# Softplus of the scan stage summed in PSUM by TensorE and copied out by ScalarE

## What is computed

```
x_conv = silu(conv(x_ssm) + conv_b)
dt = softplus(x_conv @ dt_w.T + dt_b)
dA = exp(dt[:, :, None] * A)
h = h * dA + (dt[:, :, None] * Bt[:, None, :]) * xt[:, :, None]      # 512 steps, 16 states per channel
y = einsum('bdn,bn->bd', h, Ct) + xt * D
```

## Time and profile before

| | us |
|---|---|
| median of 3 runs | 1474.12 |
| lowest, highest | 1471.44, 1475.02 |
| the profiled execution, its own time | 1474.04 |
| its span, first to last instruction | 1472.2 |
| first scan starts, last scan starts | 47.7, 673.6 |

### The profile page before, as it was taken

One profiled execution on the slowest core, in us unless ns is written; L12 is line 12 of the kernel. 1 busy time (PEld: TensorE's weight loads), 2 busy tenths in 40 slices (PEclk: granted clock), 3 DMA queues, 4 the chain that ended last, 5 costly groups with the idle time before them and its releaser, 6 DMA issues. The chain is left out here.

```text
span 1472.2 us, 17914 instructions
## 1 busy us (share of the span) xinstructions
PE 1198.7 (81%) x5074; PEld 801.4 (54%) x5074; DVE 1098.6 (75%) x1659; ACT 857.1 (58%) x1354; POOL 778.2 (53%) x519
## 2 busy tenths in 40 slices
PE   7778787887959687666139999999999999999950
PEld 3323243333424243323138888888888888888850
DVE  2889898989888898995427777777777777777743
ACT  3664646565654746431127677677767777776744
POOL 0356556777867686876632444444444444444452
PEclk8899789898968898886559999999999999999985
DMA  1443333544444443432464566556556565555537
GB/s 67 191 149 134 115 130 124 173 158 151 141 154 137 139 163 131 149 117 82 175 227 144 152 155 161 147 156 159 155 148 155 158 156 155 158 157 149 156 42 231
DMA packets 69254, 217.13 MB, mean 147 GB/s; under 512 B 7520, under 2 KB 43232, under 8 KB 56288
## 3 DMA queue, kind: packets, MB, share of 16 engines
q1 hardware_dynamic: 29664, 167.42, 31.6%
q0 software_dynamic: 26880, 36.72, 14.7%
q10 hardware_dynamic: 12672, 12.58, 2.6%
HBM read 165.54 MB, written 51.15 MB: 147 GB/s over the span
## 5 line engine op out<-in xcount | busy, mean ns | idle before, releaser
L511 PE MATMUL p_y<-read,small 128*128 128x512 f32 x512 | 297.3, 714 | 126.8 <-POOL read L1006 126.8
L850 DVE TENSOR_TENSOR_SCAN state<-decay,p_bu 128x1024 f32<-128x1024 f32 x128 | 292.3, 2283 | 33.6 <-ACT decay L677 27.9
L1432 POOL DMA_INDIRECT total<-o_v,tok x144 | 266.5, 1851 | 45.1 <-issue 44.8
L677 ACT ACTIVATE decay<-dt,scan_rate 128x511 f32<-128x511 f32 x256 | 169.2, 712 | 176.2 <-DVE state L850 175.9
L511 PEld LDWEIGHTS p_y<-read,small 128*128 128x128 f32 x512 | 104.9, 220 | 293.0 <-POOL read L1006 193.8
L1430 POOL TENSOR_TENSOR scrap<-neg_half 128x1 f32<-128x1 f32 x36 | 14.6, 405 | 356.3 <-ACT o_v L1317 353.8
L1006 POOL TENSOR_TENSOR read<-state,bc 128x1024 f32<-128x1024 f32 x64 | 150.5, 2351 | 52.4 <-DVE p_bu L841 20.3
L1294 ACT ACTIVATE gate_v<-p_g,bias 128x512 f32<-128x512 f32 x144 | 98.2, 682 | 97.1 <-PE p_up L1243 96.9
L1304 ACT ACTIVATE ah<-a_v 128x512 fp32r<-128x512 f32 x144 | 91.2, 633 | 91.7 <-DVE a_v L1378 91.7
L1006 POOL TENSOR_TENSOR read<-state,first_wh 128x1024 f32<-128x1024 f32 x32 | 75.4, 2355 | 109.7 <-DVE p_bu L841 87.8
L1367 DVE TENSOR_SCALAR up_v<-up_v 128x512 f32<-128x512 f32 x144 | 61.9, 430 | 63.7 <-ACT up_v L1297 63.6
(11 more groups left out here) (209 smaller groups left out, 3007.9 us busy)
## 6 DMA issues: line engine op xcount, KB each, us to landing
bc<-bc_rows SPq DMA_DIRECT2D x32, 1024.0 KB, 5.1
first_raw<-in_w_experts SPq DMA_DIRECT2D x19, 1668.0 KB, 6.7
raw_w<-in_w_experts SPq DMA_DIRECT2D x18, 1668.0 KB, 6.8
first_wh<-bc_rows SPq DMA_DIRECT2D x16, 1024.0 KB, 5.2
first_wl<-bc_rows SPq DMA_DIRECT2D x16, 1024.0 KB, 5.0
first_rows<-queues SPq DMA_DIRECT2D x19, 544.0 KB, 6.8
xq<-queues SPq DMA_DIRECT2D x18, 544.0 KB, 6.9
queues<-read SPq DMA_DIRECT2D x9, 544.0 KB, 4.0
```

What stands on the lines that cost most here:

```text
L511: mm = pe.matmul(p_y[h][:, :], ident[:, :], read[:, t % 4, h, :], start=False, stop=(t == SLOTS - 1))
L677: act.activation(decay[t % 2][:, h, 1:LEN], dt[s.p][:, h, 1:LEN], ACT.Exp, scale=rate[:, h, t:t + 1])\
L850: dve.tensor_tensor_scan(flat(state[t % 4][:, :, :]), flat(decay[t % 2][:, :, :]), p_bu[:, :], 0.0, ALU.mult, ALU.add).then_inc(s_state, 1)
L1432: pool.indirect_dma_start(total, bass.IndirectOffsetOnAxis(ap=tok[t.p][:, a:a + 1], axis=0), o_v[t.p][:, a, :], None, compute_op=ALU.add). ...
```

## The change

TensorE adds `relu`, `logp` and minus `rest` in one PSUM bank for each half: two matmuls through the identity and one through a new matrix `minus`, the negative identity, at t = 12, behind `in3` and ahead of that step's `sum_states`. ScalarE copies the two banks to `dt` at t = 13, ahead of the decays of t = 14 and of the gate's SiLU. Two names, `sp0` and `sp1`, join the turns of the two banks. VectorE's two sums go, with their semaphores; who waited for them now waits for the copies (`drive`, the first decays), for `rest` (GpSimd at t = 11), or for nothing (GpSimd at t = 13).

```diff
@@ -69,7 +69,7 @@
         return (["tr0", "tr1", "rt"] * d + ["in0", "in1", "cv0"] * a + ["cnt"] * d + ["cv1"] * a + ["o0", "o1"] * c
-                + ["bc", "dt0", "dt1", "in2", "in3"] * a)
+                + ["bc", "dt0", "dt1", "in2", "in3", "sp0", "sp1"] * a)
...
+    minus = sb("minus", P, at=one)
...
@@ -499,6 +500,18 @@
+        def add_softplus(r, h):
+
+            s = r.s.at(1)
+            bank, done = block(r, f"sp{h}")
+            pe.wait_ge(s_log, s.n + 1)
+            if h == 0 and r.like == Round.FIRST:
+                pe.wait_ge(s_set_dve, SET_DVE)
+            pe.matmul(bank[:, :], ident[:, :], relu[:, h, :], start=True, stop=False)
+            pe.matmul(bank[:, :], ident[:, :], logp[:, h, :], start=False, stop=False)
+            pe.wait_ge(s_rest, s.n + 1)
+            pe.matmul(bank[:, :], minus[:, :], rest[:, h, :], start=False, stop=True).then_inc(done, 1)
...
                 if r.a and t in (10, 11):
                     project(r, t - 8)
+                if r.a and t == 12:
+                    add_softplus(r, 0)
+                    add_softplus(r, 1)
...
@@ -640,8 +656,6 @@
             bank, done = full(act, r, f"dt{h}")
-            if h == 0 and r.b:
-                act.wait_ge(s_dt, r.s.n + 1)
...
+        def store_sum(r, h):
+            s = r.s.at(1)
+            bank, done = full(act, r, f"sp{h}")
+            act.activation(dt[s.p][:, h, :], bank[:, :], ACT.Copy).then_inc(done, 1)
...
-        def decays(s, t):
+        def decays(s, t, before_this=None):
 
             after(act, s_state, SLOTS * s.n + t - 1)
             if t == 0:
-                act.wait_ge(s_dt, s.n + 1)
+                for i in range(HALVES):
+                    bank, n = before_this.block(f"sp{i}")
+                    act.wait_ge(bank_read[bank], n)
...
             bank, done = full(act, r, f"tr{k}")
-            act.wait_ge(s_sum, SEQS if not r.a else r.s.n + 1)
             act.activation(x1t[:, k, :], bank[:, :], ACT.Copy).then_inc(done, 1)
...
                 if r.a and t in (11, 12):
                     store_in(r, t - 9)
+                if r.a and t == 13:
+                    store_sum(r, 0)
+                    store_sum(r, 1)
                 if r.a and t == 14:
                     silu_gate(r)
...
+        dve.tensor_scalar(minus[:, :], ident[:, :], -1.0, None, ALU.mult)
...
@@ -813,20 +837,13 @@
             dve.scalar_tensor_tensor(flat(rest[:, :, :]), flat(rest[:, :, :]), -1.0, flat(expo[:, :, :]),
                                      ALU.add, ALU.subtract).then_inc(s_rest, 1)
-            dve.wait_ge(s_log, s.n + 1)
-            dve.tensor_tensor(flat(relu[:, :, :]), flat(relu[:, :, :]), flat(logp[:, :, :]), ALU.add).then_inc(s_sum, 1)
-
-        def scan_inputs(r):
+
+        def drive(r):
 
             s = r.s.at(1)
-            dve.wait_ge(s_sum, s.n + 1)
-            dve.wait_ge(s_rest, s.n + 1)
-            dve.tensor_tensor(flat(dt[s.p][:, :, :]), flat(relu[:, :, :]), flat(rest[:, :, :]), ALU.subtract).then_inc(s_dt, 1)
-
-        def drive(r):
-
-            s = r.s.at(1)
-            dve.wait_ge(s_dt, s.n + 1)
+            for h in range(HALVES):
+                bank, n = r.block(f"sp{h}")
+                dve.wait_ge(bank_read[bank], n)
...
-                if r.a and t == 13:
-                    scan_inputs(r)
...
@@ -1046,11 +1061,9 @@
             if r.a and t == 11:
-                pool.wait_ge(s_sum, r.s.at(1).n + 1)
+                pool.wait_ge(s_rest, r.s.at(1).n + 1)
             if r.c and t == 12:
                 pool.wait_ge(s_residual, r.s.at(-1).n + 1)
-            if r.a and t == 13:
-                pool.wait_ge(s_dt, r.s.at(1).n + 1)
...
-            sp.wait_ge(s_dt, SEQS)
+            sp.wait_ge(s_u, SEQS)
```

More of the change, by code:

```diff
@@ L736, in act_stage1 @@
                 if r.next_b and t == SLOTS - 1:
-                    decays(r.s.at(1), 0)
+                    decays(r.s.at(1), 0, r)
                 if r.d and t == 0:
```

## The result

| us | before | changed |
|---|---|---|
| median of 8 runs each | 1473.49 | 1463.76 |
| lowest to highest | 1471.44 to 1475.02 | 1461.44 to 1468.57 |
| profiled execution, own time (span) | 1474.04 (1472.2) | 1463.58 (1461.7) |
| first scan, last scan start | 47.68, 673.6 | 50.72, 666.1 |

The ratio is 0.9938, 95% interval 0.9925 to 0.9951. The changed kernel is 0.6% faster; the prediction said 1473.5 us, no change. The rest of this text finds that the four terms of the prediction's sum came out and cancel nearly as it said. The 10 us came from two things that its sum carried over from the kernel before: a wait of VectorE for its own code, and waits of VectorE for a TensorE at half its clock.

What follows compares the result with a forecast made beforehand. VectorE was taken to bound the scan stage (busy 564.86 of 626.00 us). Terms -7.9 - 1.0 + 4.9 + 3.5 gave -0.5 us against 1474.04, so 1473.5 us, no change (65%), range 1468 to 1480.

Steps and rivals of the forecast that it cites:

- the four terms of the prediction's sum: First sum -7.9 us; second sum -1.0 in round 0 and +4.9 in rounds 1 to 6; first round's chain +3.5.
- Bound and method: Between first and last scan, a VectorE instruction taken out can be worth its length; ahead of the first scan, little.
- Part 1: First sum (t = 11) gone from VectorE: scan starts 1.13 us earlier in seven rounds, -7.9 us.
- Part 2: Second sum (t = 13) gone: -1.0 us in round 0; GpSimd's read holds L883, 0.81 longer in six rounds, +4.9.
- Parts 3 and 4: TensorE's sum (t = 12) and ScalarE's two copies (t = 13) are covered in steady rounds: nothing.
- Part 5: First round, nothing hides TensorE's sum and ScalarE's copies: first scan near 51.2, +3.5 us; less than +3.0 excluded.
- Rival 1: At t = 13 the shared-port lock doesn't strike, L883 goes first: 10.3 us better, 1463.2; 12%.
- Rivals 2 and 3: First round's TensorE at lower clock, 1478.6, 12%; steady-round copies so late that decays wait, 1487 if 2 us late, 5%.
- Rival 4: Removed sums pay in full and the first round hides its chain: 14.3 us better, 1459.7; 3%.
- the small edits: Extra 128x128 scaling in set-up, two new PSUM bank turns, SyncE's table load waiting for `s_u`: nothing each.
- the sum: -7.9 - 1.0 + 4.9 + 3.5 = -0.5 us against 1474.04, giving 1473.5; 1471 to 1476 for this case.
- VectorE's few waits for TensorE's router: Listed as an uncertainty: may shrink by 1 or 2 us as GpSimd reads state 12 earlier.

Runs made afterwards that it cites:

- the first experiment: Changed kernel with GpSimd at t = 13 made to wait for the second norm's moments before reading the state; 1451.13 us, ratio 0.9862.
- the one on GpSimd's wait: Kernel before without GpSimd's wait for the second sum at t = 13, both sums kept on VectorE; 1483.08 us, ratio 1.0058.
- TensorE's part alone: Kernel before plus TensorE's six matmuls and ScalarE's two copies a round into an unread tile, VectorE's sums kept; 1477.14 us, ratio 1.0029.
- the changed kernel made longer: Changed kernel with eight one-element VectorE writes, four ahead of the loop and one in each preparing round at t = 13; 1468.29 us, ratio 0.998.
- the moved kernel without stall: Kernel before with 122 one-element writes added in VectorE's set-up; 1463.91 us, ratio 0.9952.
- the best version: Changed kernel with GpSimd waiting for the moments at t = 13 and the first round's two sums back on VectorE; 1445.88 us, ratio 0.9806.

## Why the prediction was wrong, point by point

- **Bound and method: right.** The first sum taken from VectorE between the scans was worth the time by which it had held the scan (1.14 for 1.13).
- **Part 1: right**, -8.0 for -7.9.
- **Part 2: right in its mechanism**, which the first experiment and the one on GpSimd's wait show from both sides. The price in rounds 3 to 6 was 1.06 instead of 0.81, since the scan there waits 0.29 us for `neg_mean`: from the start of L900 to the scan it is 2.48 us (339.30 to 341.78), against 2.23 in round 7, from which I took it. So +5.9 for +4.9.
- **Parts 3 and 4: right** for what they cover. No scan waited for the copies. Round 0 is the exception, below.
- **Part 5: right**, +3.0 for +3.5. I had called less than +3.0 excluded; the value lies on that bound.
- **Rival 1** would have given 1463.2, within 0.6 us of what was measured, and its condition did not occur: L900 took 2.12 us. A reader with the time alone would have believed in it. Only the trace, and the run that made it true (1451.13, not 1463), tell them apart. Rivals 2 and 3 did not occur. Rival 4, that the sums pay in full, falls by the same numbers.
- **The step that failed is the one on the small edits and the sum.** It named three small edits, put them at nothing, and carried all the rest of the 1474.04 us over as it stood. Among that rest were 4.36 us of idle time on VectorE that belong to no instruction: a wait for code, which depends on where the loop lies. With the two sums gone from each round, VectorE's program is 8 instructions shorter, the loop ends at 695 instead of 703, and the wait was gone.
- **A second term was mis-sized.** Among the uncertainties stood "VectorE's few waits for TensorE's router, which may shrink by 1 or 2". In rounds 2, 5 and 7 they shrank by 5.8 us, and the traces put it down to TensorE's granted clock there, 1.00 where it had been 0.50 to 0.65. New waits of 2.9 us came in rounds 0 and 1.
- **Most of both hangs on the place of the code.** 122 idle writes gave the kernel before the same without the change: 8.5 us less among the scans, of which the intervals account for all (-4.33 at the edge, -3.55 in round 5, -1.70 in round 2, -0.50 and +0.38 in round 7, +1.12 in round 1). In the changed kernel about 5 of the 7.4 us hang on it.
- **The sum's nearness to no change was right for the kernel with its loop left in place** (ratio 0.998), as far as the noise allows to tell.

**What stays open.** Whether TensorE falls to half its clock in round 2 or round 5 follows from small shifts in time that no run here sorts out. Round 2's 3 to 4 is 5.80 in the kernel before and with 64 and 128 writes, and 4.10 in all the others, among them three that stall at the jump (TensorE's part alone, GpSimd's wait alone, the changed kernel made longer). Behind the stall, round 5's two intervals are 9.82 and 5.5 in before and with 128 writes, with 64 one is raised, and in the changed kernel made longer hardly any (8.00, 4.10). Round 1's 6 to 7 is 5.40 or over 6.5, with the clock at 1.00 in both cases; in the changed kernel VectorE waits 1.32 us there for the output projection (L537), which TensorE began 2.40 us behind the start of scan 6 instead of 1.07. Why it began later there, no run here shows. It wasn't tried either whether another placement brings more. The 3.0 us behind the last scan go with nothing: over these kernels that stretch is 794 to 799 us, in no relation to the time among the scans (before 798.6, the moved kernel without stall 795.5, the one with 128 writes 799.3, the kernel without GpSimd's wait 794.1). That a block holds 128 instructions is inferred from two shifts, of which one came out in full and one in part; it is not read from a trace.

## What to carry to other kernels

An idle stretch whose releaser is "issue", at a loop's jump back, with packets on the instruction queue beside it, was a wait for code here. "issue" alone isn't enough: the changed kernel has 8.59 us of it on VectorE ahead of the first round's `drive` (L849, at 45.70), which waits for ScalarE's second copy and started 0.10 us behind its end. Count a wait for code among what any edit of that engine may change, and before crediting an edit with a gain, run the old kernel with its code moved. Where a GpSimd instruction on a whole tile may start beside a tiny `tensor_scalar` on VectorE, put the tiny one first by a wait: that was worth 11 to 13 us here, more than the change. Read the clock of the engine that others wait for where they wait, not its mean. And what moves work off a busy engine in the steady state should leave it there in the first round, where that engine is idle (first scan 4.1 us earlier in the best version).

## What the chip showed that I had not expected

- The jump back of VectorE's loop cost 4.3 to 5.2 us when three instruction packets came in (five kernels), 3.16 with two, and nothing otherwise. Two instructions more or less decide it (701: none, 703: stall).
- TensorE pays for a pause afterwards. In the changed kernel it stood idle for 6.86 us at the start of round 0 and then ran at 1.2 GHz, half the full rate, for some 8 us (windows view: start:end, length, busy us of each engine, the granted clock third from the end):

```profile
50.70:55.00 4.30, 0.00 (x0) 0.00 (x0) 4.14 (x3) 2.47 (x4) 0.42 (x1) 0.69 0.45 191
55.00:59.00 4.00, 2.03 (x3) 0.99 (x4) 3.86 (x3) 2.30 (x4) 2.84 (x2) 0.50 0.00 0
59.00:63.00 4.00, 4.00 (x7) 1.68 (x6) 3.86 (x3) 1.51 (x3) 2.69 (x2) 0.56 0.40 129
63.00:67.00 4.00, 4.00 (x10) 1.71 (x10) 3.86 (x3) 1.83 (x3) 2.70 (x2) 1.00 0.33 133
```

  In the kernel before, the same matmuls of the first round ran at the lower rate (6.28 us for eight), lasted into round 0 and left no such pause. Here they ended early. The convolution behind the pause fell back, ScalarE waited for it, and the scan after it started 1.56 us late:

```profile
56.97 3.78 PE L524 MATMUL p_y<-read,small 128*128 128x512 f32 x4 [6.86 <-POOL read L1021]
...
72.04 0.69 ACT L640 ACTIVATE xc<-p_bank,small 128x512 f32<-128x512 f32 x1 [3.04 <-PE p_bank L492]
...
77.89 2.29 DVE L867 TENSOR_TENSOR_SCAN state<-decay,p_bu 128x1024 f32<-128x1024 f32 x1 [1.60 <-ACT decay L698]
```

- The kernel before ran between 1466.08 and 1478.0 us over 25 runs on one chip, 0.8% apart, so differences below some 4 us were read from the intervals of the traces and not from medians. The spread goes with TensorE's granted clock: the 8 runs at 0.902 or more have a median of 1467.8 us, the 17 below it 1473.4.
